# Fewer completion signals of TensorE in the four gather passes of a two-layer GNN kernel

## What is computed

```python
h = jnp.maximum(_layernorm(x, axis=-1), 0.0)
x_fwd = segment_sum(w * h[col, :128], row) / clip(deg_row, 1)     # row, col = src, dst
x_bwd = segment_sum(w * h[row, 128:], col) / clip(deg_col, 1)
x = x + concatenate([x_fwd, x_bwd], axis=-1)
```

```python
def _gat_layer(x, src, dst, W, b, a, g, beta, N, concat):
    h = x @ W.T + b
    score = (h @ a[:d])[src] + (h @ a[d:])[dst]
    e = jnp.exp(-leaky_relu(score, 0.2))
    h_prime = segment_sum(e[:, None] * h[dst], src, num_segments=N)
    ...                                            # layer norm over the features, elu
h = jnp.maximum(_layernorm(x, axis=-1), 0.0)
x = x + elu(out_layer(concatenate([head_i(h) for i in range(8)], axis=1)))
```

## Time and profile before

| | us |
|---|---|
| runs | 3297.24, 3293.55, 3287.83 (median 3293.55) |
| the profiled execution | 3294.2 |
| its span | 3292.4 |
| TensorE busy (matmuls) | 2243.2 (68%) |
| VectorE busy | 1917.8 (58%) |
| ScalarE busy | 1738.7 (53%) |
| POOL busy | 1928.0 (59%) |
| gathers of pass 1, pass 2, attention (L435) | 474.1, 450.0, and 449.2 + 446.8 for the two together, half of the slots each |

### The profile page before, as it was taken

How to read it: one execution, slowest core, us unless ns; L and a number is a source line. 1 busy time by engine, 2 the same in 40 slices (tenths; PEclk the granted TensorE clock), 3 DMA queues, 4 the chain that set the end, 5 groups by cost and what they waited for, 6 DMA issues and landing times. The chain is left out here.

```text
span 3292.4 us, 46358 instructions
## 1 busy us (share of the span) xinstructions
PE 2243.2 (68%) x14916; PEld 1669.3 (51%) x14916; DVE 1917.8 (58%) x4213; ACT 1738.7 (53%) x5133; POOL 1928.0 (59%) x1999
## 2 busy tenths in 40 slices
PE   6887778677758877343577777777767566655653
PEld 4785667567747766233343333333335445444542
DVE  8985788577747776222446666666686233333336
ACT  3995677578747776222334444344438344444444
POOL 1006666666666666666635656665645566666664
PEclk8998999799878999555688888888888777777776
DMA  2011111111141112111545656665641333333335
GB/s 60 1 41 40 40 44 43 43 45 45 45 47 44 45 44 53 47 46 47 58 140 160 169 164 173 169 170 157 168 104 33 87 92 89 91 89 90 90 90 77
DMA packets 114882, 270.48 MB, mean 82 GB/s; under 512 B 34543, under 2 KB 51670, under 8 KB 114646
## 3 DMA queue, kind: packets, MB, share of 16 engines
q0 software_dynamic: 89088, 245.53, 30.5%
q1 hardware_dynamic: 25558, 21.98, 2.1%
HBM read 250.96 MB, written 16.42 MB: 81 GB/s over the span
## 5 line engine op out<-in xcount | busy, mean ns | idle before, releaser
L435 POOL DMA_INDIRECT rows_near<-table_a,s_idx_S x464 | 474.1, 1022 | 286.0 <-issue 115.4
L435 POOL DMA_INDIRECT given<-table,s_idx_S x464 | 449.2, 968 | 301.5 <-issue 126.8
L1166 DVE TENSOR_TENSOR work<-work,bank 128x129 f32 (+2 forms) x928 | 391.0, 421 | 362.4 <-remote 163.1
L435 POOL DMA_INDIRECT rows_near<-table,s_idx_S x464 | 446.8, 963 | 252.7 <-issue 127.8
L435 POOL DMA_INDIRECT rows_near<-table_b,s_idx_D x464 | 450.0, 970 | 230.9 <-issue 101.9
L950 PE MATMUL bank<-scratch,oh 128*128 128x512 f32 x928 | 488.1, 675 | 15.9 <-DVE scratch L1413 11.7
L818 PE MATMUL bank<-rows_near,oh 128*128 128x129 f32 x1856 | 331.0, 330 | 246.6 <-issue 179.5
L647 ACT ACTIVATE e_att<-lrelu 128x32 f32<-128x32 f32 (+1 forms) x232 | 49.9, 215 | 740.6 <-DVE lrelu L1402 490.0
L818 PEld LDWEIGHTS bank<-rows_near,oh 128*128 128x128 f32 x1856 | 289.0, 234 | 282.1 <-issue 232.8
L935 PE MATMUL bank<-sort_ring,scratch 128*128 x2784 | 154.0, 169 | 329.4 <-ACT scratch L643 285.2
L538 ACT ACTIVATE scratch<-scratch,given 128x128 f16<-128x128 bf16 x840 | 284.1, 388 | 170.8 <-DVE scratch L1130 146.7
(11 more groups left out here) (222 smaller groups left out, 4799.8 us busy)
## 6 DMA issues: line engine op xcount, KB each, us to landing
rows_near<-table_a,s_idx_S POOLq DMA_INDIRECT x464
rows_near<-table_b,s_idx_D POOLq DMA_INDIRECT x464
rows_near<-table,s_idx_S POOLq DMA_INDIRECT x464
given<-table,s_idx_S POOLq DMA_INDIRECT x464
table<-scratch SPq DMA_DIRECT2D x25, 260.0 KB
table<-scratch SPq DMA_DIRECT2D x25, 128.5 KB, 3.0
xs<-in_x SPq DMA_DIRECT2D x1, 3072.0 KB
out_x<-scratch SPq DMA_DIRECT2D x24, 128.0 KB, 1.7
```

Source lines behind the costliest of these rows:

```text
L435: nc.gpsimd.indirect_dma_start(out=to, out_offset=None, in_=table[:, :], in_offset=bass.IndirectOffsetOnAxis(ap=s_idx[order][:, c:c + 1], ...
L1166: v.tensor_add(a, a, psum).then_inc(sum_free[o], 1)
```

## The change

In passes 1 and 2 only the second matmul of a pair signals: `pairs_summed` takes the place of `chunks_summed`. POOL waits once before two gathers, for both chunks that used the two slots; VectorE waits for two pairs where it waited for four chunks. In the attention passes the two signals behind the scores of q+1 and behind the transposes of q+2 become one, `turned_and_scored`, which TensorE gives after the later of the two (the transposes; for the last quads the scores). VectorE's scores of q+1 and ScalarE's copy of the transposes of q+2 wait for the same count. The signals of the sums stay two for a quad. No instruction is added, taken away or moved on any engine, and no DMA.

```diff
@@ -311,13 +311,12 @@
         tab_1 = [sem(f"tab_1{i}") for i in range(4)]
         tab_2 = [sem(f"tab_2{i}") for i in range(4)]
         gathered = [sem(f"gathered{i}") for i in range(SLOTS)]
-        chunks_summed = sem("chunks_summed")
+        pairs_summed = sem("pairs_summed")
         oh_ready = {o: sem(f"oh_ready_{o}") for o in "SD12"}
         sum_ready = {o: sem(f"sum_ready_{o}") for o in "12"}
         sum_free = {o: sem(f"sum_free_{o}") for o in "SD12"}
-        ohT_psum = {o: sem(f"ohT_psum_{o}") for o in "12"}
+        turned_and_scored = {o: sem(f"turned_and_scored_{o}") for o in "12"}
         ohT_ready = {o: sem(f"ohT_ready_{o}") for o in "12"}
-        ssrc_ready = {o: sem(f"ssrc_ready_{o}") for o in "12"}
         off_made = {o: sem(f"off_made_{o}") for o in "12"}
         z_ready = {o: sem(f"z_ready_{o}") for o in "12"}
         lrelu_ready = {o: sem(f"lrelu_ready_{o}") for o in "12"}
@@ -441,7 +440,8 @@
                 for c in range(CHUNKS):
                     if c in CUT:
                         pool.wait_ge(edges_sorted, phase * 2 + CUT.index(c) + 1)
-                    pool.wait_ge(chunks_summed, phase * CHUNKS + c + 1)
+                    if c % GP == 0:
+                        pool.wait_ge(pairs_summed, phase * GROUPS + c // GP + 1)
                     gather(table, rows0[:, c % SLOTS, 0:HALF], order, c)
 
             def gather_layer1(o, table, width):
@@ -639,7 +639,10 @@
                                          scale=-1.0, bias=ones[:, 0:1]).then_inc(oh_ready[o], 1)
 
                 def transposed(q, u):
-                    act.wait_ge(ohT_psum[o], q + 1)
+                    if isinstance(q, int) and q < 2:
+                        act.wait_ge(turned_and_scored[o], q + 1)
+                    else:
+                        act.wait_ge(turned_and_scored[o], q + 2)
                     nc.scalar.activation(ohT[:, u % 2, :], turned[u % 2], ACT.Copy).then_inc(ohT_ready[o], 1)
 
                 def weights(q, u):
@@ -815,8 +818,10 @@
                     if k == 0:
                         pe.wait_ge(sum_free[o], g + QUAD // GP)
                     pe.wait_ge(rows_scaled, phase * CHUNKS + c + 1)
-                    nc.tensor.matmul(sum0(g), oh[:, slot, :], rows0[:, slot, :],
-                                     start=(k % GP == 0), stop=(k % GP == GP - 1)).then_inc(chunks_summed, 1)
+                    last = nc.tensor.matmul(sum0(g), oh[:, slot, :], rows0[:, slot, :],
+                                            start=(k % GP == 0), stop=(k % GP == GP - 1))
+                    if k % GP == GP - 1:
+                        last.then_inc(pairs_summed, 1)
 
             for t in range(T):
                 if t == 2:
@@ -923,7 +928,7 @@
                     for k in range(QUAD):
                         upper = oh[:, u % UNROLL * QUAD + k, :].bitcast(BF16)[:, 1:2 * P:2]
                         last = nc.tensor.transpose(turned[u % 2][:, k * P:(k + 1) * P], upper, ident_bf[:, :])
-                    last.then_inc(ohT_psum[o], 1)
+                    return last
 
                 def source_scores(q, u, tiles):
 
@@ -935,7 +940,7 @@
                             last = nc.tensor.matmul(bank[2 + u % 2][:, k * heads:(k + 1) * heads], ohT[:, u % 2, k * P:(k + 1) * P],
                                                     s_parts[:, f, bass.ds(tiles[k // 2], 1), 0:heads].rearrange("p t h -> p (t h)"),
                                                     start=(f == 0), stop=(f == 2))
-                    last.then_inc(ssrc_ready[o], 1)
+                    return last
 
                 def sums(q, u):
                     for k in range(QUAD):
@@ -947,10 +952,10 @@
                             lanes, rows = oh[:, u * QUAD + k, :], m
                         else:
                             lanes, rows = m[:, 0:P], row_slots(u * QUAD + k, 1)[:, 0, 0:width]
-                        mm = nc.tensor.matmul(bank[4 + u % 2 * 2 + k // GP][:, 0:width], lanes, rows,
-                                              start=(k % GP == 0), stop=(k % GP == GP - 1))
+                        last = nc.tensor.matmul(bank[4 + u % 2 * 2 + k // GP][:, 0:width], lanes, rows,
+                                                start=(k % GP == 0), stop=(k % GP == GP - 1))
                         if k % GP == GP - 1:
-                            mm.then_inc(sum_ready[o], 1)
+                            last.then_inc(sum_ready[o], 1)
 
                 def turn(i):
                     n = 2 * UNROLL if not isinstance(i, int) or i < ROUNDS - 1 else 2 * UNROLL - 2
@@ -958,14 +963,15 @@
                     for u in range(UNROLL):
                         q = i * UNROLL + u
                         if not isinstance(i, int) or q + 1 < QUADS:
-                            source_scores(i * UNROLL + (u + 1), u + 1, tiles[2 * u:2 * u + 2])
-                        if not isinstance(i, int) or q + 2 < QUADS:
-                            transposed(i * UNROLL + (u + 2), u + 2)
+                            last = source_scores(i * UNROLL + (u + 1), u + 1, tiles[2 * u:2 * u + 2])
+                            if not isinstance(i, int) or q + 2 < QUADS:
+                                last = transposed(i * UNROLL + (u + 2), u + 2)
+                            last.then_inc(turned_and_scored[o], 1)
                         sums(q, u)
 
-                transposed(0, 0)
-                transposed(1, 1)
-                source_scores(0, 0, tile_numbers(mybir.EngineType.PE, "S", TILE_AT, 2))
+                transposed(0, 0).then_inc(turned_and_scored[o], 1)
+                transposed(1, 1).then_inc(turned_and_scored[o], 1)
+                source_scores(0, 0, tile_numbers(mybir.EngineType.PE, "S", TILE_AT, 2)).then_inc(turned_and_scored[o], 1)
                 turn(0)
                 for i in range(1, ROUNDS - 1):
                     turn(i)
@@ -1017,7 +1023,7 @@
             v.tensor_scalar(unsplit[0:32, :], ident[0:32, 0:T], 256.0, None, ALU.mult)
             link(v.tensor_copy(unsplit[32:64, :], ident[32:64, 32:32 + T]))
             dve.sem_inc(consts_made, 1)
-            dve.sem_inc(chunks_summed, SLOTS)
+            dve.sem_inc(pairs_summed, SLOTS // GP)
             dve.sem_inc(col_free, RING)
             for o in "SD":
                 dve.sem_inc(sum_free[o], SUMS0)
@@ -1154,7 +1160,7 @@
 
             def one_hots(o, phase, q):
 
-                dve.wait_ge(chunks_summed, phase * CHUNKS + q * QUAD + QUAD)
+                dve.wait_ge(pairs_summed, phase * GROUPS + 2 * (q + 1))
                 v.tensor_tensor(oh[:, q * QUAD % SLOTS:q * QUAD % SLOTS + QUAD, :],
                                 (iota_f[:, 0:P] if phase and q >= FIRST else iota_sum).unsqueeze(1).to_broadcast([P, QUAD, P]),
                                 s_lo[o][:, q * QUAD:(q + 1) * QUAD].unsqueeze(2).to_broadcast([P, QUAD, P]),
@@ -1167,7 +1173,7 @@
 
             def add_sums(o, phase, q, tiles):
 
-                dve.wait_ge(chunks_summed, SLOTS + phase * CHUNKS + QUAD * (q + 1))
+                dve.wait_ge(pairs_summed, SLOTS // GP + phase * GROUPS + 2 * (q + 1))
                 for j in range(2):
                     g = q * 2 + j
                     add_group(o, acc[o], tiles[j], g, sum0(g), SUMS0)
@@ -1391,7 +1397,7 @@
                 def scores(i, q, u):
 
                     n = QUAD * heads
-                    dve.wait_ge(ssrc_ready[o], q + 1)
+                    dve.wait_ge(turned_and_scored[o], q + 3)
                     for k in range(QUAD):
                         b = u % UNROLL * QUAD + k
                         dve.wait_ge(gathered[b], i * 16 + 16 * ((1 + int(o)) * ROUNDS + 1 + u // UNROLL))
```

## The result

| | before | after |
|---|---|---|
| median of five runs each, us | 3287.83 (3278.86 to 3297.24) | 3311.89 (3304.84 to 3314.01) |
| span of the profiled execution, us | 3292.4 | 3310.4 |
| ratio | | 1.0063 (95% interval 1.0045 to 1.008) |

A forecast was written before the change was run, and what follows sets the result against it. The prediction took POOL's gathers as the chain, delayed by TensorE signals that come late while POOL issues. From 3294 us, -30 - 10 + 14 = -26 gave 3268 us; range 3195 to 3325.

The forecast's parts named there:

- Part 1, late pass 2, -30: Passes 1 and 2, stretch 1310 to 1643: one signal per pair frees two gathers, recovering 30 of 40.4 us lost.
- The lock-step of the earlier trace: Late pass 2: gathers starting 1.41 us apart in place of 1.25, read as one TensorE signal for one gather.
- The whole of part 1, -40 in my sum: One signal per pair: -30 in late pass 2, -10 in pass 1 and early pass 2.
- The sign I had named for this: If late pass 2 keeps its 333 us, the number of signals isn't what holds POOL; the forecast expected some 303.
- Part 1, the second chunk's later end, up to +23 and +37: A pair's first gather waits for the second chunk: at worst +23 in late pass 2, +37 in pass 1 and early pass 2.
- Part 2, +14: Attention: VectorE's prompt scores wait 1.33 us more for the transposes; a quarter of 57 us charged, TensorE's sums covering the rest.
- Fewer signals shorten pauses, -65: Attention passes: 232 signals fewer, a quarter, may shorten pauses that lose 162 + 99 us; -65 at the far end.
- Rival 2: All passes: signals are held until POOL pauses and come out together, so their number is no matter; 3284 to 3303; chance 0.25.
- Rival 3: Attention: the joint signal leaves 1.3 us later and misses its turn as POOL issues again; 3347, half about 3300; chance 0.18.
- The prices of the Trainium skill: Whole kernel: 26.3 ns per increment, 18 us less for 692 signals; the other page's about 1 cycle means fewer buy nothing.

The follow-up runs named there:

- e1_pairs: The kernel before with only passes 1 and 2 changed (one signal per pair, POOL waits per pair), attention as before: 1.0006 of the time before.
- e2_joint1: The kernel before with the joint signal for scores and transposes in attention 1 alone: 1.008 of the time before, attention 1 782.5 us.
- e3_joint2: The kernel before with the joint signal for scores and transposes in attention 2 alone: 0.9997 of the time before, attention 1 753.1 us.
- e8_spare: The kernel before with three more signals per quad in attention, from the first three transposes, for which nobody waits: 1.002 of the time before.
- f1_no_pe_wait: The kernel before, but in passes 1 and 2 TensorE multiplies by a constant and POOL waits for ScalarE, not TensorE: 3532.33 us, before 3289.96.

## Why the prediction was wrong

- **Where the time is lost.** Right in what was seen: POOL's gathers are the chain, and TensorE's signals come late while POOL issues. Wrong in what was made of it. I took POOL's 40.4 us of waits in late pass 2 for the price of late signals. As far as the runs show, they are how a pace shows: with half the signals or half the rows the stretch takes some 330 us, and with 8 slots pass 2 takes 682 for 680.
- **Part 1, late pass 2, -30.** This is the first of two steps that failed. The lock-step of the earlier trace rows, read as one signal for one gather, was a gather every 1.41 us with POOL waiting out the difference. Fewer signals made 12 long stops of 89 short ones, with 35.7 us lost in place of 40.4. The whole of part 1, -40 in my sum, measured 1.0006 of the time before (e1_pairs): nothing. The sign I had named for this, late pass 2 keeping its 333 us, is what came.
- **Part 1, the second chunk's later end, up to +23 and +37.** Nothing of it shows: e1_pairs has it in its 1.0006.
- **Part 2, +14.** The second step that failed, and the one that decided the sign. I had charged the prompt scores, 34 of the 42 in attention 2, with 1.33 us for ScalarE's one-hots, and put the 88 remote ones at 0: there both signals would come together. It is the other way round. In attention 2, where the prompt scores do wait for the transposes now, the joint signal cost 0. In attention 1 it cost 15 us in the profiled executions and 0.8%, 27 us, in e2_joint1, and there the remote waits grew: from 179.1 us to 199.8, and to 225.8 in e2_joint1 from 190.7 and 197.1 in e3_joint2 and e1_pairs. Signals that are held back don't come together; the later one can come a gather later, 1.36 us at the place shown for 0.24 us between the matmuls. And I had asked only whether TensorE's sums cover the delay: in attention 1 POOL waits for VectorE's messages, so a later score delays the gathers whether TensorE is busy or not.
- **Fewer signals shorten pauses, -65.** They don't; e8_spare puts 696 more at some 7 us.
- **The rivals.** Rival 2 describes passes 1 and 2, with about the same loss in fewer, longer waits, and the time of attention 2. Rival 3 is what decided the sign: a joint signal that misses its turn, with a chance of 0.18. I had looked for it in attention 2, and it was in attention 1. The two together are the result, inside the range (3195 to 3325) but on the other side of the forecast.
- **The prices of the Trainium skill.** "TensorE: Matmul & The Clock Gate", section "The cost: per-tile semaphore tail", has increments serialize, with 26.3 ns for each in its model of the tail; an estimate by that page is 18 us less for 692 fewer. No such gain came. What e8_spare gives for signals that are added is about 10 ns each, an estimate (7 us for 696). "Advanced Engine Details and Errata", section "DMA Bandwidth Details", with about one cycle, spoke for no gain from fewer signals, and there the runs agree (1.0006 in e1_pairs).

## What to carry to other kernels

Before you shorten a wait, ask whether the total of the waits follows their number: change the ring's size or the count of signals, and if many short waits turn into few long ones with the same sum, something else sets the pace. When two signals become one, price the later consumer by who waits behind it, on every engine, and not by the microseconds between the two producers. And where a wait must be, put work that is ready in front of it: the two adds ahead of the late score were worth 11 us.

## What was not expected of the hardware

While gathers were issued back to back, 1.25 us apart, TensorE's completion signals reached the other engines late: a quad's four in each 22.40 us, and still late 26 us after 212 gathers (f1_no_pe_wait), when the rows of all of them had landed. With gathers 1.44 us apart they were prompt in late pass 2 and in attention 1, though not in attention 2, and a kernel whose POOL does more was faster by 0.2%. A pace of about 1.40 us per gather, independent of the rows fetched, fits late pass 2 in all its forms and the end of f1_no_pe_wait's gathers. It doesn't explain attention 2, nor the losses at 1.33 us. What has this pace was not found.
